# A down product that lags two tiles behind the up product in the routed stage

## Time and profile before

| | |
|---|---|
| median of three runs | 934.22 us (933.71 to 942.43) |
| profiled execution, its own time | 940.29 us |
| its span | 938.6 us |
| granted TensorE clock over the span | 0.993 |
| TensorE busy | 842.6 us (90%) |
| TensorE weight loads | 697.0 us (74%) |
| VectorE busy | 651.0 us (69%) |
| ScalarE busy | 482.1 us (51%) |
| GpSimd busy | 175.2 us (19%) |
| routed stage, first up product to last chunk's first | 731.84 to 854.77 us |

### The profile page before, as it was taken

How to read it: one execution, slowest core, us unless ns; L and a number is a source line. 1 busy time by engine, 2 the same in 40 slices (tenths; PEclk the granted TensorE clock), 3 DMA queues, 4 the chain that set the end, 5 groups by cost and what they waited for, 6 DMA issues and landing times. The chain is left out here.

```text
span 938.6 us, 14797 instructions
## 1 busy us (share of the span) xinstructions
PE 842.6 (90%) x3976; PEld 697.0 (74%) x3976; DVE 651.0 (69%) x1343; ACT 482.1 (51%) x848; POOL 175.2 (19%) x221
## 2 busy tenths in 40 slices
PE   0029999998999999999999999999999799998997
PEld 0018888886788888887888888878888677777885
DVE  7986867753578777655686885546775677773774
ACT  5416564633455646345556544534553476765441
POOL 1010000011110000112000001210222666653550
PEclk9999999999999999999999999999999899999999
DMA  8232333359533333494433335565794366666975
GB/s 183 56 101 68 113 94 91 85 104 175 126 110 114 92 90 90 105 213 86 136 112 90 92 99 102 110 182 157 136 209 150 113 210 211 210 203 250 310 225 168
DMA packets 121086, 130.72 MB, mean 139 GB/s; under 512 B 9968, under 2 KB 83744, under 8 KB 120508
## 3 DMA queue, kind: packets, MB, share of 16 engines
q1 hardware_dynamic: 112076, 104.80, 42.3%
q0 software_dynamic: 8784, 25.11, 9.0%
q10 hardware_dynamic: 160, 0.02, 0.0%
HBM read 106.91 MB, written 22.98 MB: 138 GB/s over the span
## 5 line engine op out<-in xcount | busy, mean ns | idle before, releaser
L498 PE MATMUL up<-xs,w1hi 128*128 128x512 f32 x512 | 203.8, 398 | 6.8 <-ACT xs L800 6.0
L499 PE MATMUL up<-xs,w1hi 128*128 128x512 f32 x512 | 200.1, 391 | 0.0
L500 PE MATMUL up<-xs,w1lo 128*128 128x512 f32 x512 | 199.9, 391 | 0.0
L539 PE MATMUL acc<-w2hi,hhi 128*128 128x512 f32 x504 | 196.4, 390 | 3.9 <-ACT w2hi L743 3.9
L540 PE MATMUL acc<-w2lo,hhi 128*128 128x512 f32 x504 | 196.4, 390 | 0.0
L738 ACT ACTIVATE hhi<-up,b_col 128x512 fp32r<-128x512 f32 x128 | 88.4, 690 | 163.5 <-PE up L500 137.2
L926 DVE TENSOR_TENSOR hlo<-hf,hhi 128x512 fp32r<-128x512 f32 x128 | 88.0, 688 | 102.0 <-ACT hf L741 61.0
L543 PE MATMUL acc<-w2hi,hlo 128*128 128x512 f32 x504 | 135.7, 391 | 0.0
L498 PEld LDWEIGHTS up<-xs,w1hi 128*128 128x128 f32 x512 | 96.6, 189 | 27.5 <-ACT xs L800 7.0
L539 PEld LDWEIGHTS acc<-w2hi,hhi 128*128 128x128 f32 x504 | 94.6, 188 | 23.9 <-ACT w2hi L743 4.3
L500 PEld LDWEIGHTS up<-xs,w1lo 128*128 128x128 f32 x512 | 96.5, 189 | 20.6
(11 more groups left out here) (227 smaller groups left out, 1109.3 us busy)
## 6 DMA issues: line engine op xcount, KB each, us to landing
w_raw<-in_L_ffn_sw SPq DMA_DIRECT2D x256, 256.0 KB, 3.1
expert_rows<-ysb SPq DMA_DIRECT2D x47, 256.0 KB, 2.4
X<-in_x SPq DMA_DIRECT2D x16, 256.0 KB, 6.7
vin<-in_ctx SPq DMA_DIRECT2D x16, 256.0 KB, 8.3
xn_rows<-kn POOLq DMA_DIRECT2D x16, 256.0 KB, 7.8
e2raw<-in_L_ffn_ew SPq DMA_DIRECT2D x16, 256.0 KB, 4.9
ew_sb<-in_L_ffn_ew SPq DMA_DIRECT2D x16, 256.0 KB, 7.5
out<-X SPq DMA_DIRECT2D x12, 256.0 KB, 4.5
```

Of the source, the lines that this page charges most:

```text
L498: nc.tensor.matmul(o, lhs[0], rhs[0], start=start, stop=False)
L499: nc.tensor.matmul(o, lhs[0], rhs[1], start=False, stop=False)
L500: return nc.tensor.matmul(o, lhs[1], rhs[0], start=False, stop=stop)
L539: nc.tensor.matmul(acc[t][:], hh, w2hi[:, slot], start=first or again, stop=False)
```

## The change

The routed stage's loops are written one tile ahead. PE does T(2) and up(1) ahead of its loop, and in round s T(s+3), up(s+2), down(s). `rf` and `rhi` get three places, since their content now lives longer. ACT and DVE get their loops turned: what stood at the end of round s stands at the start.

```diff
+    RB = 3
@@ buffers
-        rf = sb("rf", [P, 2, P], where=routed_mem)
-        rhi = sb("rhi", [P, 2, P], f32r, routed_mem)
+        rf = sb("rf", [P, RB, P], where=routed_mem)
+        rhi = sb("rhi", [P, RB, P], f32r, routed_mem)
@@ tensor: routed_down
-                i = s % 2
+                i, h = s % 2, s % RB
...
-                splits(y_bank[i][:], (rhi[:, i], rlo[:, i]), (e2hi[:, e], e2lo[:, e]), True, True).then_inc(ry, 1)
+                splits(y_bank[i][:], (rhi[:, h], rlo[:, i]), (e2hi[:, e], e2lo[:, e]), True, True).then_inc(ry, 1)
@@ tensor: the loop
             routed_up(0)
+            routed_T(2)
+            routed_up(1)
...
             for s in range(SLOT_TILES):
+                if s + 3 < SLOT_TILES:
+                    routed_T(s + 3)
                 if s + 2 < SLOT_TILES:
-                    routed_T(s + 2)
-                if s + 1 < SLOT_TILES:
-                    routed_up(s + 1)
+                    routed_up(s + 2)
                 routed_down(s)
@@ scalar
-                need(act, ry, s - 1)
+                need(act, ry, s - RB + 1)
...
             routed_h(0)
+            routed_x(2)
             for s in range(SLOT_TILES):
-                if s + 2 < SLOT_TILES:
-                    routed_x(s + 2)
+                if s + 1 < SLOT_TILES:
+                    routed_h(s + 1)
+                if s + 3 < SLOT_TILES:
+                    routed_x(s + 3)
                 if s:
                     routed_y(s - 1)
-                if s + 1 < SLOT_TILES:
-                    routed_h(s + 1)
@@ vector
-                need(dve, rhl, s - 1)
+                need(dve, rhl, s - RB + 1)
...
             routed_w1(2)
+            routed_x(2)
+            routed_sum(1)
             routed_h(0)
+            routed_w1(3)
             for s in range(SLOT_TILES):
-                if s + 2 < SLOT_TILES:
-                    routed_x(s + 2)
-                if s + 1 < SLOT_TILES:
-                    routed_sum(s + 1)
-                if s + 3 < SLOT_TILES:
-                    routed_w1(s + 3)
                 if s + 1 < SLOT_TILES:
                     routed_h(s + 1)
+                if s + 3 < SLOT_TILES:
+                    routed_x(s + 3)
+                if s + 2 < SLOT_TILES:
+                    routed_sum(s + 2)
+                if s + 4 < SLOT_TILES:
+                    routed_w1(s + 4)
```

More of the change, by code:

```diff
@@ L875, in routed_h @@
             def routed_h(s):
-                i = s % 2
+                i = s % RB
                 b = bslot[:, s:s + 1]
@@ L1376, in routed_sum @@
                 dve.wait_ge(rup, s + 1)
-                need(dve, rhl, s - 1)
-                V.tensor_reduce(rf[:, i], r_bank[i][:, 0:2 * P].rearrange("p (a n) -> p n a", a=2), AX.X, ALU.add)\
+                need(dve, rhl, s - RB + 1)
+                V.tensor_reduce(rf[:, s % RB], r_bank[i][:, 0:2 * P].rearrange("p (a n) -> p n a", a=2), AX.X, ALU.add)\
                     .then_inc(rsm, 1)
             def routed_h(s):
-                i = s % 2
+                i = s % RB
                 dve.wait_ge(rhh, s + 1)
@@ L1385, in routed_h @@
                 need(dve, ry, s - 1)
-                V.tensor_tensor(rlo[:, i], rf[:, i], f(rhi[:, i]), ALU.subtract).then_inc(rhl, 1)
+                V.tensor_tensor(rlo[:, s % 2], rf[:, i], f(rhi[:, i]), ALU.subtract).then_inc(rhl, 1)
             routed_w1(0)
```

## The result

The changed kernel takes **942.09 us** (median of 20 runs, 939.36 to 948.92) against 936.1 us of the kernel before (20 runs, 932.16 to 942.43): a ratio of **1.0064, 95% interval 1.0042 to 1.0086**, slower by 6.0 us. The profiled execution took 947.1 us, with a span of 945.4 against 938.6 and the same granted clock, 0.993.

The account below looks back on a forecast made before the run. The prediction took a ring through DVE and ACT, without PE, to bound the routed stage. Meetings +9.9 and start -2.6 gave +7.3 us on 934.22, so 941.5 us, range 931 to 944.5.

Parts of the forecast that it names:

- The ring: Routed stage: sum, gelu, gelu, cast, x, sum through DVE and ACT sets the 2.51 us round; the change adds 0.
- PE's new phase: In each round PE waits at the up product, which starts once x is ready, some 0.45 us earlier.
- The meeting: POOL's weight cast starts 0.02 us ahead of DVE's remainder, delaying it; 38 rounds grow by 0.26 us: +9.9 us.
- The slack: In each round x, held by ACT's cast, leaves 0.20 us of remainder delay that costs nothing.
- rival 1: DVE's remainder gets in ahead of POOL's cast, so only the gain at the start is left: 931.6 us; chance 0.27.
- POOL wins even a tie: Against rival 1: POOL goes first when both start together, read from a gather at 761.94 where DVE pays 0.05.
- The start: First tiles of the stage: PE fills its gap before 734.81, gaining one tile: -2.6 us, bounds -2.0 and -3.8.
- The upper bound, -3.8: At the stage's start, -3.8 us if the clock stays up and the tile gained is one of 3.84 us.
- The end: Last tile of the routed stage: still sum, gelu, gelu, remainder, down, copy, then the last chunks: 0.
- The sum: Whole kernel: +9.9 - 2.6 = +7.3 us, profiled 947.6 us; median 941.5 us, 0.8% slower.

Follow-up runs that it names:

- the kernel at 2.22: Changed kernel with ACT's gelus behind its cast for x and DVE's remainder behind the next sum and weight remainder: 927.99 us (0.9827), again 925.28 (0.9848).
- The kernel with one more product: Changed kernel plus one superfluous product behind each up product, whose end releases POOL's cast: 933.87 us against 937.16 of the kernel before (0.9968).
- The three kernels of the meeting: Changed kernel with POOL's cast waiting for the remainder (937.68 us), with one superfluous product behind each up product (933.87), or with the cast in two halves (941.07).
- PE's two products alone: Kernel before, with only the transpose of tile 2 and up product of tile 1 brought forward: 940.0 us against 941.26 (0.9978).
- the order alone: Kernel before, down product still one tile behind, with gelus and remainder behind x(s+3) on ACT and DVE: 1025.82 us against 937.16.
- the kernel with four places: The kernel at 2.22 with four places for `e1hi`, so POOL's cast of tile k waits for up product k-4: 919.48 us against 937.16 (0.9791).

## Why the prediction came out

**The ring, 0: right.** The links x, sum, gelu, gelu, cast take 1.90 us for 1.91, the wait of 9.8 us at PE is gone and nothing was gained by it. That the order of DVE and ACT sets the round was shown from the other side, by the kernel at 2.22: there the gelus are out of the ring and the round shrinks.

**PE's new phase: right.** It stands at each up product; the wait is listed as "issue", not under DVE's x, yet the load follows the start of x by 0.75 (776.18 to 776.93), for the 0.76 forecast.

**The meeting: right in kind and in order, a little too dear.** The cast comes 0.02 to 0.03 ahead, in all 41 rounds that have the meeting, none mixed; the remainder takes 0.73 for the 0.75 forecast. A round grew by 0.23 for 0.26. The slack measured 0.21 for 0.20, so the difference is the 0.02 of the remainder and 0.01 of slack. There were more meetings than forecast, 41 for 38: they begin three tiles sooner, with PE rid of the low clock at 737.1; the last four remainders met none, as forecast. 40 of the 41 lie between the sums of tiles 3 and 45, and 40 x 0.227 is the 9.06 us of the table. Forecast were +9.9.

That the sign came out is in part luck. The leads were 0.018 to 0.034 us, the smallest lead with which a cast won in any of these traces is 0.017, and one of 0.008 lost. The prediction held against rival 1 that "POOL wins even a tie", which it had read from a gather beside a weight remainder. For gathers that is so (one won even 0.037 behind), but a cast 0.003 behind a weight remainder lost. So the argument was worth less than it seemed. The kernel with one more product, its cast 0.12 us later against the remainder, is rival 1, made: its stage is 9 us shorter.

**The start: -3.0 for -2.6, and its reason half right.** I had said that PE keeps the tile gained and stays at the low level until 741.0. It left it at 737.1. The upper bound, -3.8, was for a level that stays up throughout, but priced the tile at 3.84, which is a tile at the lower level. The three kernels of the meeting had the full level throughout and gained 3.2; the changed kernel gained the same 3.2, less 0.2 for the first meeting, with the level low for 3.4 us. So in the order of the change the lower level cost nothing, and the shorter stretch of it is not where the gain came from. PE's two products alone gave 1.4, with the level low as long as before. The Trainium skill's "TensorE: Matmul & The Clock Gate", section "What's actually happening", by which activity lifts the throttle, fits the traces with the whole change, in which the stretch at the lower level is shorter or missing; but the kernel with only the gap filled kept its 6.8 us, so a filled gap alone did not lift the level sooner here.

**The end, 0: wrong by 0.49.** Two places of the last tiles:

```profile
856.68 0.40 ACT L887 ACTIVATE rf<-rf,bslot 128x128 f32<-128x128 f32 x1
...
857.53 0.29 DVE L1390 TENSOR_TENSOR rlo<-rf,rhi 128x128 fp32r<-128x128 f32 x1 [1.42 <-ACT rhi L884]
...
859.04 1.05 ACT L893 COPY ysb<-acc 128x512 f32<-128x512 f32 x2
...
859.85 0.50 PE L499 MATMUL acc<-e2hi,rhi 128*128 x1 [0.86 <-ACT ysb L893]
```

The remainder of the last tile but one starts 0.45 after the second gelu's end (857.08), where 0.09 is usual: that is 0.36. Why is open. Of what it waits for, the profile shows nothing that late; the same late start is in the three kernels of the meeting (5.81 us from sum to chunks in each), two of which have no meeting, so that isn't it, and the kernel with PE's start alone does not have it. The other 0.13 is the last down product, which starts 0.63 behind the last remainder instead of 0.50. It waits for ACT's copy of the product two tiles before (that bank must be free), and this copy now stands behind the last gelus and not ahead of them.

**The sum.** +9.1 - 3.0 + 0.5 = +6.6 in the stage for a forecast of +7.3, the dearer end and the deeper start offsetting each other in part; the profiled execution took 947.1 for 947.6. The median of 941.5 came to 942.09 by two things that offset each other: the measured difference is 6.0, 1.3 less, and the 20 runs of the kernel before have a median 1.9 above that of the three I started from.

## What to carry to other kernels

A wait on a busy engine is worth nothing as long as the round is a ring through other engines; add up one round link by link, start to start, before taking a wait for the bound. If the links add up to the round, change their order: here the lag alone cost 0.6%, the order alone 9% (one run), and both together gained 1.5 to 1.7%. And when an edit shifts one engine's phase, lay the new starts of POOL and DVE side by side: a single product more or less decided some 9 us.

## What the runs showed of the hardware

- Who holds the memory that DVE and POOL share is decided by a few hundredths of a microsecond: with the cast 0.02 to 0.03 ahead, the DVE remainder takes 0.73 for 0.29; with the remainder 0.09 ahead, it keeps its 0.29 and the cast takes 0.68 for 0.61. The Trainium skill's "SBUF — State Buffer", section "SBUF: two separate sides", calls it an exclusive lock, held for the whole instruction, with the other side fully blocked. The one who starts second does pay in these rows, but each side pays less than the other has left, by some 0.15 (DVE) and 0.13 (POOL: 0.20 left, 0.07 paid).
- A cast of half the size on POOL takes 0.40 us, not half of 0.61.
- A gather on POOL costs the DVE weight remainder beside it little (0.73 for 0.68 in the earlier trace rows, 0.76 at most), but is itself stretched from 0.97 to 1.48 where the weight remainder is far enough ahead. With the weight remainder 0.039 us ahead it was stretched (744.31), with 0.037 it was not (754.21 us in the kernel with four places); in the fast kernel the stretched one came again (742.75 us, 1.48). A cast beside a remainder is decided elsewhere: it won with 0.017 us of lead and lost with 0.008.
- In the stage in which PE stood idle for a third of the time the granted clock went to and fro between its two levels, 0.79 in the mean, and the ring's rounds went from 3.88 us to as much as 5.1.
- Whether the level falls at the start of the stage changes between traces of kernels with the same order of PE there: from 733.7 to 737.1 us in the changed kernel, not at all in three others.
